# Softmax attention of a four-layer kernel: scores on four PSUM banks instead of two, and other places for transposes, output chunks, a reciprocal and a residual

## What is computed

```python
h = layernorm(x)                                  # (8, 512, 512)
q = h @ w_q + b_q ; k = ctx @ w_k + b_k ; v = ctx @ w_v + b_v
q, k, v = (t.reshape(8, 512, 16, 32) for t in (q, k, v))
scores = einsum('bqhd,bkhd->bhqk', q, k) / sqrt(32)
x = x + einsum('bhqk,bkhd->bqhd', softmax(scores), v).reshape(8, 512, 512) @ w_o + b_o
```

## Time and profile before

| | us |
|---|---|
| median of 3 runs | 1703.21 (1697.96 to 1706.17) |
| the profiled execution | 1706.38 |
| its span | 1704.5 |
| mean granted clock of TensorE | 0.971 |
| TensorE, VectorE, ScalarE, GpSimd busy | 1528.9, 1190.5, 1121.4, 1022.1 |

### The profile page before, as it was taken

One profiled execution on the slowest core, in us unless ns is written; L12 is line 12 of the kernel. 1 busy time (PEld: TensorE's weight loads), 2 busy tenths in 40 slices (PEclk: granted clock), 3 DMA queues, 4 the chain that ended last, 5 costly groups with the idle time before them and its releaser, 6 DMA issues. The chain is left out here.

```text
span 1704.5 us, 28818 instructions
## 1 busy us (share of the span) xinstructions
PE 1528.9 (90%) x8836; PEld 671.3 (39%) x8836; DVE 1190.5 (70%) x1438; ACT 1121.4 (66%) x1895; POOL 1022.1 (60%) x738
## 2 busy tenths in 40 slices
PE   5999878998999974899999999999999968999998
PEld 3545433443444431333333334343433313444443
DVE  4978898997989755666676767676676646655552
ACT  5667598887888743566666666666666656566662
POOL 4767437766778722566666666666666664554442
PEclk9989899999999996999999999999999988999999
DMA  8411000000000112121211112111211100010001
GB/s 310 147 64 46 1 1 1 1 1 1 0 1 1 46 51 80 32 57 34 53 34 46 47 33 54 32 54 33 56 37 35 53 30 25 25 49 25 25 25 50
DMA packets 61226, 72.18 MB, mean 42 GB/s; under 512 B 15312, under 2 KB 40784, under 8 KB 60624
## 3 DMA queue, kind: packets, MB, share of 16 engines
q1 hardware_dynamic: 57968, 62.36, 12.4%
q10 hardware_dynamic: 3168, 8.78, 1.3%
HBM read 37.40 MB, written 8.39 MB: 27 GB/s over the span
## 5 line engine op out<-in xcount | busy, mean ns | idle before, releaser
L1594 DVE TENSOR_REDUCE s_mx<-bank 128x2 f32<-128x1024 f32 x256 | 301.6, 1221 | 207.4 <-PE bank L1719 207.4
L1471 ACT ACTIVATE s_E<-bank 128x512 f32<-128x512 f32 x512 | 281.6, 596 | 204.2 <-PE bank L1735 198.0
L1355 POOL TENSOR_TENSOR s_E<-s_E 128x1024 f32<-128x1024 f32 x128 | 302.5, 2375 | 92.5 <-ACT s_E L1471 92.5
L1735 PE MATMUL bank<-s_QA,s_KA 97*128 97x512 f16 x512 | 179.3, 389 | 28.0 <-DMA s_QA<-s_mrow 7.5
L1908 POOL TENSOR_TENSOR sm_cx<-m_xf,sm_cx 128x512 f16<-128x512 f32 x60 | 84.1, 1407 | 104.5 <-ACT sm_cx L1950 104.5
L1743 PE MATMUL bank<-s_E,s_V 128*32 128x512 f32 x1024 | 139.0, 615 | 4.6 <-ACT s_E L1471 2.8
L1076 PE MATMUL bank<-sm_zz,w1raw 128*128 128x512 f16 x256 | 99.3, 388 | 28.7 <-DVE sm_cx L963 15.5
L1598 DVE RECIPROCAL bank<-bank 128x256 f32<-128x256 f32 (+1 forms) x66 | 112.7, 1708 | 17.2 <-PE bank L1751 17.2
L1099 PE MATMUL bank<-f_w2q,w2raw 128*128 128x512 f16 x512 | 121.8, 379 | 0.6 <-DVE w2raw L951 0.3
L773 POOL TENSOR_TENSOR sm_wkv<-sm_wkv,sm_cx 128x511 f32<-128x511 f32 x48 | 66.1, 1377 | 90.1 <-DVE sm_wkv L963 80.6
L767 POOL TENSOR_TENSOR w1raw<-w1raw,sm_cx 128x512 f32<-128x512 f32 x88 | 115.6, 1334 | 2.3 <-ACT sm_cx L855 2.3
(11 more groups left out here) (268 smaller groups left out, 4038.2 us busy)
## 6 DMA issues: line engine op xcount, KB each, us to landing
sm_cx<-in_ctx SPq DMA_DIRECT2D x16, 768.0 KB, 4.5
X<-in_x SPq DMA_DIRECT2D x8, 1024.0 KB, 6.8
s_QA<-sm_cx SPq DMA_DIRECT2D x256, 32.0 KB, 1.9
out_x<-X SPq DMA_DIRECT2D x8, 1024.0 KB, 4.3
s_KA<-sm_cx SPq DMA_DIRECT2D x244, 32.0 KB, 1.9
w1raw<-in_w ACTq DMA_DIRECT2D x1, 4096.0 KB, 14.2
w2raw<-in_w ACTq DMA_DIRECT2D x1, 4096.0 KB, 27.9
s_QA<-s_qkh SPq DMA_DIRECT2D x128, 32.0 KB, 1.8
```

The costliest lines, as they stand in the source:

```text
L1355: e.tensor_tensor(into, into, other, ALU.add).then_inc(s_sum.sem, 1)
L1471: e.activation(E[:, SLOT[k] + h, :], SC[u % 2][:, :], ACT.Exp, scale=1.0 / float(np.sqrt(DH)))\
L1594: e.tensor_reduce(mx[:, 2 * i:2 * i + 2, q], MAXED[i][:, :, :], AX.X, ALU.max).then_inc(s_red.sem, 1)
L1735: e.matmul(SC[u % 2][:, :], KA[0:MROW + 1, m, h, t * P:(t + 1) * P], QA[0:MROW + 1, m, h, :], start=True, stop=True).then_inc(s_sc.sem, 1)
```

## The change

Scores of a step that has a next group go to banks 0 to 3, by u % 4 (`s_bank`); without one they keep banks 0 and 1. With a next group score u no longer waits for exponential u-2; instead h = 0 waits for the first reduction of the quarter and h = 2 for the second. `rows` writes into `MX[0]` instead of `MX[2]`, and waits for exponential 12 of the step before. Outputs at the end in banks 2 and 3 wait for the last reduction and the exponentials of the groups before the last. The tables: T_AT from 9, 11, 13, 15 to 8, 11, 11.5, 14; in m = 1 output (0,2) from 11 to 9 and (1,0) from 11.5 to 12; in m = 2 residual 2 from unit 10 to 9 and the second reciprocal from 8 to 10. The loops over T_AT take fractional keys: ScalarE's high part of 11.5 stands after exponential 11, VectorE's low part after the reductions of unit 12.

```diff
--- before.py
+++ after.py
@@ -1179,14 +1179,14 @@
     Q_AT = ((-1, -1, 1, 3), (-1, -1, 1, 3), (0, 1, 2, 3), (0, 1, 2, 3))
     K_AT = ((3, 5, 7), (5, 7, 7), (7, 7.5, 11), (3, 3.5, 5))
     V_AT = ({2: (7, 7.5, 9, 11), 3: (11.5, 11.5, 13, 15)}, {}, {}, {0: (7, 7, 9, 11), 1: (11, 11.5, 13, 15)})
-    T_AT = (9, 11, 13, 15)
-    O_AT = ({}, {3: ((0, 0),), 7.5: ((0, 1),), 11: ((0, 2), (0, 3)), 11.5: ((1, 0),), 13: ((1, 1),), 15: ((1, 2),)},
+    T_AT = (8, 11, 11.5, 14)
+    O_AT = ({}, {3: ((0, 0),), 7.5: ((0, 1),), 9: ((0, 2),), 11: ((0, 3),), 12: ((1, 0),), 13: ((1, 1),), 15: ((1, 2),)},
             {-1: ((1, 3),), 3: ((2, 0),), 5: ((2, 1),), 7: ((2, 2),), 9: ((2, 3),), 11: ((3, 0),), 11.5: ((3, 1),), 13: ((3, 2),)},
             {-1: ((3, 3),)})
-    RES_AT = ({}, {12: 0}, {0: 1, 10: 2}, {0: 3})
+    RES_AT = ({}, {12: 0}, {0: 1, 9: 2}, {0: 3})
     STATS_AT, MOMENTS_AT, NORM_AT = {0: (0, 1, 2), 4: (3,)}, 4, (0, 1, 2, 3)
     DN_TILE, AN_AT = (1, 1, 1, 2), 12
-    RC_AT = ({4: (0,), 8: (1,)}, {4: (0,), 10: (1,)}, {4: (0,), 8: (1,)}, {8: (0,), 12: (1,)})
+    RC_AT = ({4: (0,), 8: (1,)}, {4: (0,), 10: (1,)}, {4: (0,), 10: (1,)}, {8: (0,), 12: (1,)})
     MIX_UNITS, XF_UNITS = (2, 4, 8, 10, 13), (3, 5, 9, 11)
     SLOT = (0, 4, 8, 4)
     END_BANK, END_UNITS = (6, 7, 2, 3), (8, 10, 12, 14)
@@ -1220,8 +1220,9 @@
         part = [flat(KA[:, 0:1, :, :])[:, k * S:(k + 1) * S] for k in range(2)]
         xf = [flat(KA[:, 1:2, :, :])[:, k * S:(k + 1) * S] for k in range(2)] + [qkf[:, :]]
         mixed_h = [(wq[:, 0:KD * D], wq[:, KD * D:]), (wkv[:, 0:KD * D], wkv[:, KD * D:2 * KD * D])]
-        SC, MX, MAXED, NUM, DEN, R6, R7 = banks[0:2], banks[0:4], pairs[0:2], banks[4], banks[5], banks[6], banks[7]
-
+        MX, MAXED, NUM, DEN, R6, R7 = banks[0:4], pairs[0:2], banks[4], banks[5], banks[6], banks[7]
+
+        s_bank = lambda u, nxt: MX[u % (4 if nxt else 2)]
         q_bank = lambda m: 6 if m in (1, 2) else 7
         v_bank = lambda m: 7 if m == 1 else 6
 
@@ -1454,7 +1455,7 @@
                 e.activation(V[:, m, :, :], (bank or banks[v_bank(m)])[:, :].rearrange("p (t d) -> p t d", t=TT), ACT.Copy, scale=1 / WS)\
                     .then_inc(s_V.sem, 1)
 
-            def exponential(b, m, u):
+            def exponential(b, m, u, nxt):
 
                 k, h = divmod(u, 4)
                 if k == 0:
@@ -1468,7 +1469,7 @@
                     s_sum.wait(e, b, 4 * m + 1 + h // 2)
                     s_pv.wait(e, b, 16 * m + 8)
                 e.wait_ge(s_sc.sem, s_sc.count(b, 16 * m + u + 1))
-                e.activation(E[:, SLOT[k] + h, :], SC[u % 2][:, :], ACT.Exp, scale=1.0 / float(np.sqrt(DH)))\
+                e.activation(E[:, SLOT[k] + h, :], s_bank(u, nxt)[:, :], ACT.Exp, scale=1.0 / float(np.sqrt(DH)))\
                     .then_inc(s_ex.sem, 1)
 
             def numerators(b, m):
@@ -1486,7 +1487,7 @@
             def rows(b, m):
                 s_mT.wait(e, b, m + 1)
                 s_md[(m - 1) % NG].wait(e, b, 1 if m else 0)
-                e.activation(mrow[:, :], MX[2][0:4 * TT, 0:P], ACT.Copy, scale=-1.0 / MS).then_inc(s_mrow.sem, 1)
+                e.activation(mrow[:, :], MX[0][0:4 * TT, 0:P], ACT.Copy, scale=-1.0 / MS).then_inc(s_mrow.sem, 1)
 
             def shifted(c):
                 s_p.wait(e, B - 1, 2 * NG - 1)
@@ -1528,12 +1529,13 @@
                 if m == 2 and not last:
                     context(b + 1, 2)
                 for u in range(UNITS):
-                    exponential(b, m, u)
-                    if m == 1 and u in T_AT:
-                        if last:
-                            shifted(T_AT.index(u))
-                        else:
-                            high(b + 1, T_AT.index(u), R7)
+                    exponential(b, m, u, nxt)
+                    for c in range(KD):
+                        if m == 1 and u <= T_AT[c] < u + 1:
+                            if last:
+                                shifted(c)
+                            else:
+                                high(b + 1, c, R7)
                     if last and m == 3 and u in MIX_UNITS:
                         mix(MIX_UNITS.index(u))
                     if u == 3 and m == 3:
@@ -1561,7 +1563,7 @@
             wa(e, (0,))
             stack(e, 0, 0, 1)
             for m in range(2):
-                values(0, m, SC[m])
+                values(0, m, MX[m])
             queries(0, 1, 0, R6)
             queries(0, 1, 1)
             wa(e, (1,))
@@ -1635,8 +1637,9 @@
                         residual(b - 1, RES_AT[m][u])
                     if nxt and u % 4 == 0:
                         maxima(*nxt, u // 4)
-                    if m == 1 and not last and u in T_AT:
-                        low(b + 1, T_AT.index(u), R7)
+                    for c in range(KD):
+                        if m == 1 and not last and u - 1 < T_AT[c] <= u:
+                            low(b + 1, c, R7)
                     if div:
                         for i in RC_AT[m].get(u, ()):
                             reciprocals(*div, i, S // 2)
@@ -1720,8 +1723,9 @@
                 last.then_inc(s_mx.sem, 1)
 
             def rows(b, m):
+                s_ex.wait(e, b, 16 * m - 3)
                 e.wait_ge(s_red.sem, s_red.count(b, 2 * TT * (m + 1)))
-                e.transpose(MX[2][0:4 * TT, 0:P], mx[:, :, :].rearrange("p h q -> p (h q)"), ident[:, :]).then_inc(s_mT.sem, 1)
+                e.transpose(MX[0][0:4 * TT, 0:P], mx[:, :, :].rearrange("p h q -> p (h q)"), ident[:, :]).then_inc(s_mT.sem, 1)
 
             def score(b, m, u, nxt):
                 t, h = divmod(u, 4)
@@ -1729,10 +1733,11 @@
                     for w in range(2):
                         e.wait_ge(s_sh[m][w].sem, s_sh[m][w].count(b, NSH))
                     e.wait_ge(s_md[m].sem, s_md[m].count(b, 1))
-                if nxt and h == 0:
-                    e.wait_ge(s_red.sem, s_red.count(nxt[0], 2 * (TT * nxt[1] + t) + 1))
-                s_ex.wait(e, b, 16 * m + u - 1)
-                e.matmul(SC[u % 2][:, :], KA[0:MROW + 1, m, h, t * P:(t + 1) * P], QA[0:MROW + 1, m, h, :],
+                if nxt and h % 2 == 0:
+                    e.wait_ge(s_red.sem, s_red.count(nxt[0], 2 * (TT * nxt[1] + t) + h // 2 + 1))
+                if not nxt:
+                    s_ex.wait(e, b, 16 * m + u - 1)
+                e.matmul(s_bank(u, nxt)[:, :], KA[0:MROW + 1, m, h, t * P:(t + 1) * P], QA[0:MROW + 1, m, h, :],
                          start=True, stop=True).then_inc(s_sc.sem, 1)
 
             def attend(b, m, t):
@@ -1764,10 +1769,9 @@
                 elif q == 0:
                     s_al.wait(e, b, c + 1)
                 if c == 0:
-                    if i == 2:
-                        s_mrow.wait(e, b, NG)
-                    elif i == 3:
+                    if i < 4:
                         e.wait_ge(s_red.sem, s_red.count(b, 2 * TT * NG))
+                        e.wait_ge(s_ex.sem, s_ex.count(b, 16 * (NG - 1)))
                     else:
                         take(i)
                     reader[i] = (s_res, b, q + 1)
```

## The result

| | before | after |
|---|---|---|
| median of the runs, us | 1704.69 (4 runs, 1697.96 to 1707.64) | 1661.63 (4 runs, 1659.90 to 1663.50) |
| the profiled execution, us | 1706.38 | 1659.90 |
| its span, us | 1704.5 | 1657.9 |
| ratio after to before | | 0.9753, 95% interval 0.9721 to 0.9785 |

The kernel is 43 us faster; 1667 was forecast, with a range of 1656 to 1684.

The account below looks back on a forecast made before the run. TensorE, 95% busy in the attention loop, was taken to bound the kernel, with stalls on exponentials and VectorE. Gains of 29.8 (six batches), 4.0 (first) and 3.6 (last) sum to 37.4 us: 1667 forecast, range 1656 to 1684.

Parts of the forecast that it names:

- What bounds the kernel: Attention loop: TensorE 95% busy; a quarter (four scores) has the floor maxima, reduction, score, four exponentials; stalls come on top.
- Four banks: Scores 2 and 3 wait for the second reduction; quarters ending on TensorE lose stalls, typically 0.32 us, exponential-bound ones nothing.
- the hand-over: From second reduction to score 2: 0.13 us, so start at 3.00; the other bound, 0.05, gave 2.93.
- The row transpose: Moved to bank 0 with a wait for exponential 12, over some 2 us before TensorE comes there: costs nothing.
- Step m=1: Third quarter 6.70 to 5.57 us, last 7.10 to 7.15; score 12 waits until 2.82; gain 1.75 per batch.
- Step m=2: Output (3,0) no longer waits for residual 2; third quarter 5.94 to 4.89 us, last 5.28 to 5.33; gain 1.34.
- Who else sets the pace: VectorE, ScalarE, GpSimd rise to 72, 68, 70% busy in the loop; SyncE's copies are early; costed at nothing.
- First and last batch: Attention batches outside the loop: first gains 4.0 us (2 to 6), last gains 3.6 (2 to 4.5).
- The sum: Whole kernel: six loop batches 29.8 us, first batch 4.0, last 3.6, together 37.4; predicted time 1667.
- The banks give nothing: Rival: score 3's stall only moves, and only the new places in m=1 and m=2 pay; 1691 us, chance 0.10.
- VectorE jams: Rival: in m=1, low(1) or residual(0) falls another reciprocal, 1.76 us, behind; 1679 us, chance 0.14.
- By the clock: Rival: the 1.0 us wait before score 12 drops TensorE's granted clock in m=1 of every batch; 1738 us, chance 0.03.

Follow-up runs that it names:

- e_rows2: Changed kernel with the row transpose back in bank 2, waiting for exponential 14 instead of 12; 1664.41 us in one run, batch 86.11.
- e_unroll: Kernel before the change with TensorE's loop over batches written out, so its waits have constant counts; 1712.75 us in one run.
- r_after: The changed kernel as it is, run again on one chip beside a kernel with further table moves; 1661.76 us, ratio to before 0.9745.
- e_banks: Changed kernel's four banks with all tables as before the change; 1677.95 us, ratio to before 0.9865, batch 88.28.
- e_light: Changed kernel, but second reciprocal and residual 0 of m=1 work on 8 columns only; 1654.56 us in one run, batch 85.46.
- e_best: Changed kernel with output (1,0) of m=1 before score 12, last transpose after score 15, second reciprocals of m=1, m=2 at unit 12; 1662.72 us, batch 86.02.

## Why the prediction was right

*What bounds the kernel.* Right. The quarter with its two ends, TensorE's work or the four exponentials, gave the change quarter by quarter. The forecast quarters sum to 86.87, the measured to 86.10, and no quarter is off by more than 0.15. One addition is off by 0.02: 6.52 and 0.65 give 7.17 for the last quarter of m=1, not 7.15. And the first batch of the loop isn't like the others: it took 92.36 before and 87.44 after, a gain of 4.9 where the others gained 5.7.

*Four banks.* Right in mechanism, off in one size. Score 3 follows by 0.22 everywhere, the third quarter of m=0 is held by exponentials, though it was forecast to stay at 4.71 and gained 0.15. The term that was mis-sized is the hand-over: 0.13 after a releaser was taken from the kernel before, where I had the bound 0.05 beside it; it is 0.06 now behind exponentials and behind the second reduction. Where score 2 waits for that one, it starts at 2.93, the lower bound, not at 3.00. The quarters came out shorter than forecast by 0.15 in the third of m=0, 0.12 and 0.14 in the last ones of m=1 and m=2, and 0.07 in four others; with the small rest 0.77 per batch. About 0.45 of it is the hand-over. The rest has other causes: in the third quarter of m=0 each exponential comes a little sooner, in the last of m=1 the maxima follow the start of the row by 0.59 and not by 0.65, in the last of m=2 the two reductions take 2.28 and not 2.36, and in the last of m=0 batch 3 of the kernel before, at 6.33, was itself 0.05 above its neighbours. The timeline before held the hint for the hand-over: batch 7, written out, already had 0.05.

*The row transpose* costs nothing: right, shown by e_rows2.

*Step m=1.* T(1) at 4.32 (forecast 4.33), reductions at 1.47 (1.47), score 12 at 2.75 (2.82), quarters 5.56 and 7.03 (5.57 and 7.15). Reading VectorE's order, and adding the distances between starts, found the wait that replaced the one removed.

*Step m=2.* Third quarter 4.89 as forecast, last one 5.19 (5.33). The wait of score 14 for the second reduction, forecast until 3.20, did not come: the reduction ends at 3.00, and TensorE reaches the score at 3.07.

*Who else sets the pace.* Nobody, as forecast, but for one: the copy of the negated row, which was thought early because SyncE waits for the row, holds score 0 of m=1 for 1.0 us in the first batch of the loop, and in e_unroll in five of six batches.

*First and last batch.* 5.1 and about 4.1 (4.0 and 3.6). The first is good to 1 us only: batch 0 of the same changed kernel took 92.8 us in one profile and 91.8 in that of r_after. In the first the granted clock still falls, one step later than before: the windows of the kernel before for 710.3 to 718.5, and of the kernel after for 721.9 to 730, show it at 0.71 and 0.79. TensorE was busy for 4.5 of the 7.8 us before the one, and for 10.6 of the 14.3 us before the other.

```profile
702.50:710.30 7.80, 4.52 (x26) 1.86 (x25) 5.49 (x7) 4.10 (x9) 4.46 (x3) 0.87 0.04 9
710.30:718.50 8.20, 8.05 (x38) 2.29 (x39) 2.73 (x3) 4.34 (x9) 4.51 (x2) 0.71 0.18 44
```

```profile
721.90:730.00 8.10, 8.07 (x43) 2.55 (x43) 2.36 (x2) 3.96 (x8) 4.63 (x3) 0.79 0.18 44
707.60:721.90 14.30, 10.59 (x66) 2.69 (x66) 11.01 (x9) 9.18 (x18) 9.30 (x6) 1.00 0.17 41
```

*The sum.* Loop 33.5 (29.8 forecast), first batch 5.1, last 4.1: 42.7 where 37.4 were forecast. So 3.7 of the 5.3 that were missing lie in the loop's terms above and the rest in the two rougher ones. The profiled pair differs by 46.6, because the layers ahead took 5.4 less (first maxima at 636.4, not 641.8) and the part behind 1.4 more. The first is scatter, as the other kernels show.

*The rivals.* "The banks give nothing" fell with e_banks (3.5 of 5.7 us per batch). The Trainium skill's page "TensorE: Matmul & The Clock Gate", section "HAM oscillation — how this bites in real kernels", tells of another kernel, to which double-buffering gave no further gain; taken as a rule, that did not carry over to this one, and e_banks decides. "VectorE jams" did not come in its dear form, but e_light shows that the row of work cost 0.65 per batch. "By the clock": four banks left the loop at 1.00, with a wait of 1.0 us in every m=1. So the swinging clock that the same page of the Trainium skill tells of in "A second HAM failure mode: psum-queue depth-cycling" does not show in this kernel's loop.

## What to carry to other kernels

When two results compete for banks, look for banks that are already free by the time: here the maxima's four banks stand empty from each reduction on, and using them took out 27 waits per batch without a bank more. Judge each stretch by which of its two or three ends comes last, and check an edit by the length of the repeating unit, which is good to 0.1 us where the time of the whole scatters by up to 9 in five executions. An engine that idles a quarter of the time can still be the one whose order decides: work in front of a reduction is paid by all that wait for it, and moving it one quarter on (e_best) may only move the bill.

## What was new about the hardware

A TensorE instruction held by an exponential follows its end by 0.05 to 0.06 us where TensorE's loop is written out (e_unroll, batch 7) and in the loop of the changed kernel, and by 0.13 us in the loop of the kernel before. Why the two loops differ is argued above, not shown. Behind the negated row it is 0.41 us in both loops and 0.25 written out. Writing the loop out saved 0.5 us in the one batch where nothing else changed, and in the five others a wait of about 1.2 us for the copy of the negated row took more than that back.
